# Order of the gate tiles in the up-projection stage of a quantized attention and feed-forward kernel

## What is computed

```python
x = act_qdq(x)                                   # x: layer-normed, 4096 rows of 512
up = act_qdq(x @ lpbq_dequant(w_up).T)           # 4096 x 1536
gate = act_qdq(x @ lpbq_dequant(w_gate).T)       # 4096 x 1536
sig = fixed_qdq_u16(jax.nn.sigmoid(gate))
gate = act_qdq(gate * sig)
o = act_qdq(gate * up)
return o @ lpbq_dequant(w_down).T
```

## Time and profile before

| | us |
|---|---|
| median of 3 runs (lowest, highest) | 898.39 (894.74, 899.74) |
| the profiled execution | 900.64 |
| its span, first to last instruction | 898.8 |
| TensorE busy in the span | 862.7 (96%) |
| VectorE busy | 691.9 (77%) |
| ScalarE busy | 586.1 (65%) |
| GpSimd busy | 194.9 (22%) |
| mean granted TensorE clock | 0.987 of full |
| DMA moved | 236.56 MB, mean 263 GB/s |

### The profile page before, as it was taken

How to read it: one execution, slowest core, us unless ns; L and a number is a source line. 1 busy time by engine, 2 the same in 40 slices (tenths; PEclk the granted TensorE clock), 3 DMA queues, 4 the chain that set the end, 5 groups by cost and what they waited for, 6 DMA issues and landing times.

```text
span 898.8 us, 11953 instructions
## 1 busy us (share of the span) xinstructions
PE 862.7 (96%) x4108; PEld 426.4 (47%) x4108; DVE 691.9 (77%) x965; ACT 586.1 (65%) x712; POOL 194.9 (22%) x170
## 2 busy tenths in 40 slices
PE   7999879999999999999999979999799989999998
PEld 5777554444444444444444424444344434444443
DVE  4889985565646559589997859757899997999992
ACT  2378776786654456599997758952789965555430
POOL 0099949499100196000000000000000000000000
PEclk9999979999999999999999989999999999999999
DMA  9822219756987549999459984799997887989872
GB/s 348 330 95 95 117 70 311 204 189 186 296 265 278 194 169 216 269 382 362 165 178 356 356 287 154 281 372 387 291 406 275 276 325 270 359 306 390 312 305 100
DMA packets 118402, 236.56 MB, mean 263 GB/s; under 512 B 47952, under 2 KB 57168, under 8 KB 116304
## 3 DMA queue, kind: packets, MB, share of 16 engines
q1 hardware_dynamic: 117200, 231.77, 73.4%
q10 hardware_dynamic: 1152, 4.19, 1.2%
HBM read 130.55 MB, written 95.42 MB: 251 GB/s over the span
## 4 chain that ended last, share of the span: by engine, by line
PE 66%; POOL 8%; DVE 7%; DMA 7%; issue 6%; ACT 4%; SPq 1%; ACTq 0%; DVEq 0%; POOLq 0%
PE ps L1097 23%; PE ps L1034 21%; PE ps L1150 14%; PE ps L1050 4%; PE ps L1177 3%; POOL big L866 2%; DMA big<-in_L_ffn_w_gate_dram 2%; DVE big L1948 2%; DVE big L1941 2%; DMA big<-gate_park 2%; DMA product_park<-big 1%; POOL big L823 1%; POOL big L817 1%; ACT big L1471 1%; PE ps L1167 1%
## 5 line engine op out<-in xcount | busy, mean ns | idle before, releaser
L1097 PE MATMUL ps<-big 128*128 (+1 forms) x1152 | 251.6, 382 | 6.2 <-ACT big L1195 6.2
L1195 ACT ACTIVATE big<-ps 128x1024 f32<-128x1024 f32 (+2 forms) x154 | 126.2, 830 | 138.6 <-PE ps L1034 62.4
L1034 PE MATMUL ps<-big 128*128 (+1 forms) x864 | 186.6, 379 | 0.3 <-DVE big L1725 0.3
L1097 PEld LDWEIGHTS ps<-big 128*128 128x128 f16 x1152 | 113.3, 98 | 144.4 <-issue 10.2
L1034 PEld LDWEIGHTS ps<-big 128*128 128x128 f16 x864 | 84.4, 98 | 102.3 <-DVE big L1725 0.8
L1150 PE MATMUL ps<-big 128*128 128x512 f16 x576 | 126.7, 383 | 2.3 <-DVE big L1969 2.3
L808 POOL PARTITION_ALL_REDUCE small<-small x8 | 3.0, 369 | 462.6 <-DVE small L1910 184.9
L1770 DVE TENSOR_REDUCE small<-big 128x1 f32<-128x1024 f32 x36 | 43.8, 1217 | 70.7 <-ACT big L1195 70.6
L1150 PEld LDWEIGHTS ps<-big 128*128 128x128 f16 x576 | 56.7, 99 | 71.7 <-issue 5.1
L1131 PE MATMUL ps<-big 128*128 128x512 f16 x384 | 85.1, 384 | 4.9 <-ACT big L1478 4.9
L1880 DVE CUSTOM_DVE_ANT_0 big<-big,small 128x1024 f32<-128x1024 int16 x48 | 61.6, 1284 | 7.3 <-DVE small L1874 0.5
(11 more groups left out here) (118 smaller groups left out, 1220.1 us busy)
## 6 DMA issues: line engine op xcount, KB each, us to landing
big<-up_park SPq DMA_DIRECT2D x90, 512.0 KB, 7.0
big<-gate_park SPq DMA_DIRECT2D x48, 512.0 KB, 6.5
up_park<-big SPq DMA_DIRECT2D x48, 512.0 KB, 5.0
gate_park<-big SPq DMA_DIRECT2D x36, 512.0 KB, 2.7
sign_park<-big SPq DMA_DIRECT2D x36, 256.0 KB, 2.7
big<-in_x_dram SPq DMA_DIRECT2D x8, 1024.0 KB, 18.2
x_park<-big SPq DMA_DIRECT2D x8, 1024.0 KB, 4.0
product_park<-big SPq DMA_DIRECT2D x16, 512.0 KB, 5.9
```

Source lines behind the costliest of these rows:

```text
L1034: mm = nc.tensor.matmul(unit_banks(n)[:, j], WG[:, x, a, k % 2, o:o + P], XT[:, g, b, k], start=(k == 0 and a + b == 0), stop=(k == KC - 1 ...
L1097: mm = nc.tensor.matmul(ps[:, b + j], WU[:, a, t // 3, k, t % 3], XT[:, g, c, k], start=(k == 0 and a + c == 0), stop=(k == KC - 1 and c = ...
L1195: return nc.scalar.activation(dst, src, ACT.Copy)
```

## The change

The bench tiles are worked from step 14 on, mixed with the shelf tiles, by a table `WORK` that gives the tile of each step. Signals count steps in place of tiles. `BENCH`, `BACK` and `HOLD` get other place numbers. A refill is issued two units after the unit that issued its product's store, in one run behind the shelf fetches and ahead of the stores of its unit. And the whole preparation of the up weights moves by one unit: loads, block maxima and scales by one flat unit, their high and low halves and the transposes by one quad.

```diff
-UP_AT = (1, 2, 3, 4)
-LOAD_AT = 27
-BLOCKS_AT = (29, 30)
-SCALE_AT = (31, 33)
+UP_AT = (0, 1, 2, 3)
+LOAD_AT = 26
+BLOCKS_AT = (28, 29)
+SCALE_AT = (30, 32)
...
-BENCH = (0, 1, 2, 3, 0, 1, 2, 3, 4, 5, 0, 1, 2, 3, 4, 5, 6, 7, 0, 1, 2, 3, 4, 5, 8)
+BENCH = (0, 1, 0, 1, 2, 3, 0, 1, 2, 3, 0, 1, 4, 5, 2, 3, 0, 4, 1, 6, 7, 5, 2, 3, 8)
 PARKED = 16
-BACK = (9, 6, 7, 0, 1, 2, 3, 4, 5, 8, 10, 11, 9, 6, 7, 0)
+BACK = (9, 0, 4, 1, 6, 7, 5, 2, 3, 8, 10, 11, 9, 0, 4, 1)
+BENCH_TURN = (14, 15, 20, 21, 23, 24, 26, 27, 29, 30, 32, 33, 34, 35, 36, 37) + tuple(range(39, 48))
...
-HOLD = (1, 2, 3, 4, 5, 8, 0, 6, 7, 9, 10, 11, 12, 13, 14, 15)
+HOLD = (6, 7, 5, 2, 3, 8, 0, 4, 1, 9, 10, 11, 12, 13, 14, 15)
 N_LD = 8
+
+
+def work_order():
+    kept = iter(range(KEPT))
+    return tuple(KEPT + BENCH_TURN.index(p) if p in BENCH_TURN else next(kept) for p in range(NU))
+
+
+WORK = work_order()
...
             def refill(i):
                 x = BENCH[i - KEPT]
                 later = [j for j in range(i + 1, NU) if j >= KEPT and BENCH[j - KEPT] == x]
-                if later:
-                    sp.wait_ge(p_st[(i - KEPT) % 4], 16 * ((i - KEPT) // 4) + 16)
-                    fetch_gate(later[0])
+                sp.wait_ge(p_st[(i - KEPT) % 4], 16 * ((i - KEPT) // 4) + 16)
+                fetch_gate(later[0])
...
             def park_product(i):
-                sp.wait_ge(a_mx, i + 1)
+                sp.wait_ge(a_mx, WORK.index(i) + 1)
...
                 if n:
                     park_up(n - 1)
                     next_gates(n)
-                for i in steps(n):
-                    if KEPT <= i < KEPT + PARKED:
-                        park_product(i)
-                    if KEPT < i <= KEPT + PARKED:
-                        refill(i - 1)
+                for t in steps(n - 2) if n > 1 else ():
+                    if KEPT <= WORK[t] < KEPT + PARKED:
+                        refill(WORK[t])
+                for t in steps(n):
+                    if KEPT <= WORK[t] < KEPT + PARKED:
+                        park_product(WORK[t])
...
-            def gate_abs(i):
+            def gate_abs(t):
+                i = WORK[t]
                 gate_fetched(act, i)
-                need(act, a_mx, i - 1)
-                nc.scalar.activation(g_abs[:, i % 2], place(i), ACT.Abs, scale=col["ginv"]).then_inc(abs_d, 1)
+                need(act, a_mx, t - 1)
+                nc.scalar.activation(g_abs[:, t % 2], place(i), ACT.Abs, scale=col["ginv"]).then_inc(abs_d, 1)
```

More of the change, by code:

```diff
@@ L1417, in take_up, with gate_int, sigmoid @@
                 copy(up_place(n), ps[:, b:b + 2].rearrange("p b w -> p (b w)")).then_inc(u_ev, 1)
-            def gate_int(i):
+            def gate_int(t):
+                i = WORK[t]
                 gate_fetched(act, i)
-                need(act, sig_d, i - 1)
-                nc.scalar.activation(g_int[:, i % 2], place(i), ACT.Copy, scale=col["ginv"]).then_inc(qact_d, 1)
-            def gate_abs(i):
+                need(act, sig_d, t - 1)
+                nc.scalar.activation(g_int[:, t % 2], place(i), ACT.Copy, scale=col["ginv"]).then_inc(qact_d, 1)
+            def gate_abs(t):
+                i = WORK[t]
                 gate_fetched(act, i)
-                need(act, a_mx, i - 1)
-                nc.scalar.activation(g_abs[:, i % 2], place(i), ACT.Abs, scale=col["ginv"]).then_inc(abs_d, 1)
-            def sigmoid(i):
-                if i % 3 == 0:
-                    act.wait_ge(qact_d, i // 3 + 1)
-                else:
-                    act.wait_ge(qdve_d, 2 * (i // 3) + i % 3)
-                act.wait_ge(abs_d, i + 1)
-                nc.scalar.activation(place(i), g_int[:, i % 2], ACT.Sigmoid, scale=col["gsc"]).then_inc(sig_d, 1)
+                need(act, a_mx, t - 1)
+                nc.scalar.activation(g_abs[:, t % 2], place(i), ACT.Abs, scale=col["ginv"]).then_inc(abs_d, 1)
+            def sigmoid(t):
+                if t % 3 == 0:
+                    act.wait_ge(qact_d, t // 3 + 1)
+                else:
+                    act.wait_ge(qdve_d, 2 * (t // 3) + t % 3)
+                act.wait_ge(abs_d, t + 1)
+                nc.scalar.activation(place(WORK[t]), g_int[:, t % 2], ACT.Sigmoid, scale=col["gsc"]).then_inc(sig_d, 1)
             def settle(q):
@@ L1449, in _ @@
                 if n < A_UNITS:
-                    for i in steps(n):
-                        if i % 3 == 0:
-                            gate_int(i)
-                        gate_abs(i)
-                        sigmoid(i)
+                    for t in steps(n):
+                        if t % 3 == 0:
+                            gate_int(t)
+                        gate_abs(t)
+                        sigmoid(t)
                 if n == B_UNIT:
@@ L1864, in up_max, with gate_int, sig_int, gate_product @@
                                         apply_absolute_value=True).then_inc(u_mx, 1)
-            def gate_int(i):
+            def gate_int(t):
+                i = WORK[t]
                 gate_fetched(dve, i)
-                need(dve, sig_d, i - 1)
-                nc.vector.tensor_scalar(g_int[:, i % 2], place(i), col["ginv"], None, ALU.mult).then_inc(qdve_d, 1)
-            def sig_int(i):
-                dve.wait_ge(sig_d, i + 1)
-                need(dve, a_mx, i - 1)
-                nc.vector.tensor_scalar(s_int[:, i % 2], place(i), 65536.0, 65535.0, ALU.mult, ALU.min).then_inc(r_d, 1)
-            def gate_product(i):
-                dve.wait_ge(abs_d, i + 1)
-                dve.wait_ge(r_d, i + 1)
-                s = i % 2
-                nc.vector.tensor_tensor_reduce(place(i), g_abs[:, s], s_int[:, s], 1.0, scol[:, s:s + 1],
+                need(dve, sig_d, t - 1)
+                nc.vector.tensor_scalar(g_int[:, t % 2], place(i), col["ginv"], None, ALU.mult).then_inc(qdve_d, 1)
+            def sig_int(t):
+                dve.wait_ge(sig_d, t + 1)
+                need(dve, a_mx, t - 1)
+                nc.vector.tensor_scalar(s_int[:, t % 2], place(WORK[t]), 65536.0, 65535.0, ALU.mult, ALU.min).then_inc(r_d, 1)
+            def gate_product(t):
+                dve.wait_ge(abs_d, t + 1)
+                dve.wait_ge(r_d, t + 1)
+                s = t % 2
+                nc.vector.tensor_tensor_reduce(place(WORK[t]), g_abs[:, s], s_int[:, s], 1.0, scol[:, s:s + 1],
                                                ALU.mult, ALU.max, scol[:, s:s + 1]).then_inc(a_mx, 1)
@@ L1902, in _ @@
                 if n < A_UNITS:
-                    for i in steps(n):
-                        if (i + 1) % 3 and i + 1 < NU:
-                            gate_int(i + 1)
-                        sig_int(i)
-                        gate_product(i)
+                    for t in steps(n):
+                        if (t + 1) % 3 and t + 1 < NU:
+                            gate_int(t + 1)
+                        sig_int(t)
+                        gate_product(t)
                 if n == B_UNIT:
```

## The result

| us | before | changed |
|---|---|---|
| median (lowest to highest) of 6 runs each | 899.10 (894.74 to 901.0) | 889.23 (888.38 to 890.84) |
| the profiled execution | 900.64 | 889.12 |
| its span | 898.8 | 887.3 |
| up stage, first to last matmul | 257.66 | 248.65 |
| DMA moved, mean GB/s | 236.56 MB, 263 | 236.56 MB, 267 |

The ratio of the runs is 0.990, 95% interval 0.9877 to 0.9924: 1.0% faster. In the changed kernel the lines are moved by some 10: the up matmul is L1106, the copies of up tiles L1204, the gate integer tiles L1432 (ScalarE) and L1881 (VectorE), the low halves L1669, the combines L1827.

What follows compares the result with a forecast made beforehand. The prediction took TensorE as the bound, with its up stage stopped by ScalarE's late copy. -9.02 for the up stage and +0.6 for the quads gave -8.4 us: 892.2 profiled, 890.0 as median, range 886 to 896.

Steps and rivals of the forecast that it cites:

- The up stage, -9.02 us: Up stage: TensorE's 6.23 us stop behind ScalarE's late copy and 2.8 us of low clock both go, -9.02 us.
- The cover of 14.5 us: Up stage: TensorE may run three units, 15.5 us, ahead; less the copy's 1.0 us, 14.5 us of ScalarE's lateness are covered.
- The relation of the prediction: Up stage: TensorE stops for what ScalarE's lateness exceeds 14.5 us; 20.7 us of waits give 6.2.
- The lateness left: Up stage, after the change: ScalarE 4.7 us late from transfer backlog, 12.7 at most with late refills; no stop.
- The 8.4 us at tile 39: Up stage: ScalarE's 8.4 us wait for tile 39, fetched one unit before its work, goes with the mixed order.
- ScalarE's sooner start, 0 in the sum: Start of the up stage: sooner up weights take 0 to 3.20 us off ScalarE's lateness; TensorE gains 0.
- The low halves, +0.6 us: Quads: sooner low halves fall more under GpSimd's rounding; stops of 1.9 us in place of 1.25, +0.6 us.
- rival 2: Quads: every pair of low halves in quads 0 to 2 is slow, +2.5 us, 892 us; chance 0.08.
- The second part: Units 33 to 47: up tile 38's copy, delayed by product fetches, stays hidden with 8 us left before unit 42.
- Rival 3: Second part of the up stage: a late up store or full DMA stops TensorE there instead, about 896; chance 0.06.
- Rival 4: Up stage: two units are too short for refills, gate tiles come late, the kernel is slower, 905.8; chance 0.06.
- Profiled against median: Whole kernel: the runs' median lies 2.25 us below the profiled execution, so 892.2 us profiled becomes 890.0.

Runs made afterwards that it cites:

- e11: The changed kernel with ScalarE's absolute values of step 30 (unit 20) made 16 times more, as lateness put in by hand; 901.3 us in one execution.
- e6: The changed kernel with refills three units behind the store in place of two; 897.39 us against 899.02 for the kernel before, ratio 0.9983.
- e5: The kernel before, old order and places, with only the refills moved two units behind their store; 901.15 us against 899.02, ratio 1.0032.
- e9: The changed kernel with ScalarE's absolute values of step 30 (unit 20) made 10 times more, as lateness put in by hand; 889.17 us in one execution.
- e1: The kernel before with only the places of tiles 39 to 42 changed, so tile 39's late fetch goes; 893.21 us against 897.54, ratio 0.9956.
- e3: The changed kernel with the up weights back at their old units; 889.41 us against 897.54 for the kernel before, ratio 0.9918.
- e2: The kernel before with only the up weights prepared a unit sooner; 894.42 us against 897.54, ratio 0.9971.
- e7: The changed kernel with loads, maxima and scales of the up weights at their old units, halves still sooner; 893.26 us against 899.02 before, ratio 0.9926.
- e8: The changed kernel with the up weights' halves back in quads 1 to 4, loads and scales still sooner; 890.0 us against 899.02 before, ratio 0.9885.
- e4: The changed kernel with refills one step behind the store, as in the kernel before; 890.79 us against 897.54 for the kernel before, ratio 0.9924.
- e12: The kernel before with new places for tiles 39 to 42 and up weights a unit sooner, old order and refills; 892.47 us against 898.43, ratio 0.9932.
- e10: The changed kernel with ScalarE's absolute values of step 30 (unit 20) made 13 times more, as lateness put in by hand; 896.38 us in one execution.

## Why the prediction was right, point by point

Forecast 890.0 (886 to 896), measured 889.23; 0.81 on faster. The mechanism is the one forecast, the stop behind ScalarE's late copy and the clock behind it. One term had the wrong sign, and some luck is in the closeness (last point).

- **The up stage, -9.02 us.** Right to the tenth: 257.66 to 248.65. That the stop was 6.2 us of lateness over the cover, and that a stop of this size costs 2.3 to 2.8 us of clock on top, is shown by e11, where both were made by hand; but a stop of 5.41 us (e6) cost 1.8, and e5, with two stops, paid twice, so "2.8 once" was one value of several. The cover of 14.5 us held in e9 to e11. The relation of the prediction was looser: it took the sum of ScalarE's waits for its lateness. In the kernel before this fits (20.7 waited, 20.6 us late at tile 26), because the 3.3 us left of the late start and the 0.33 us a unit won back cancel. In e5 and e6 the sums, 23.7 (23.1 for gate tiles, 0.6 for up stores) and 21.5 us, less 14.5 would give 9.2 and 7.0 us; the stops were 6.98 and 5.41.
- **The lateness left.** I had counted 4.7 us of backlog; the lateness is 4.6. That they meet is partly chance: 1.4 of the 4.6 us are there at every second tile from 16 to 24, and the one wait for a transfer is 3.1. The count for the kernel before was wrong: its SP code has 44 transfers in units 16 to 25, not 42, so 66.9 us in 51.8, and with tile 39 the sum is 23.5, not 20.4, against 20.7 waited. The count gives the direction; it was 2.8 us off there. The other estimate, a refill up to 0.5 us late at the median and 8 us in sum, was too dark: ScalarE never waited for a gate tile. The refills were issued sooner than I took from the old queue (where the up store stood behind a refill's wait), and product stores landed in 3.6 us at the median. The upper end of 12.7 us was not needed.
- **The 8.4 us at tile 39.** Right that it goes, wrong as a clean term: e1 gave back 3 of them as waits for up stores. The two causes, backlog and short distance, were not additive. Which share of the 20.7 us each has stays open.
- **ScalarE's sooner start, 0 in the sum.** Right for the changed kernel (e3), where TensorE has no stop to shorten. ScalarE's first gate instruction no longer waits for a transfer, and it began 4.2 us behind the stage's start in place of 5.2. The sooner weights by themselves were worth 3.1 us (e2), some 0.8 of it in the quads, which I would not have given them.
- **The low halves, +0.6 us.** This step failed in sign: the quads became 0.85 us shorter. I priced the pairs by their number under GpSimd, 0.6 us a quad, 1.9 us of stops in sum; they were 0.23, with eight long halves in place of the nine I had counted. The profiles show that one pair of 3.8 us makes the stop, and that ending the rounding 5 us sooner takes its usual place away (e7, e8). The error is 1.5 us. The Trainium skill, "SBUF — State Buffer", section "Who interferes with whom", calls the shared ports an exclusive lock. The durations agree that the two engines get in each other's way (a half takes 0.68 us alone and up to 1.96 under GpSimd); that the lock is exclusive no run here shows. It doesn't say which pair TensorE would feel, and rival 2 did not come.
- **The second part.** 8 us of margin forecast, 8.6 found. Rival 3 was seen only in e1 and e2 (0.8 to 1.0 us), where the first stop goes but ScalarE stays late.
- **Rival 4** needed the refill one unit later still (e6). Its 905.8 us is a slip: 898.4 + 16.2 - 9.0 is 905.6.
- **Profiled against median.** I took the profiled execution's 2.25 us over the median for a constant. It isn't one: the changed kernel's profiled execution took 889.12, at its median. Why the profile before was a long one is not shown. The low clock at the start of its down projection made that start 0.8 to 1.4 us longer than in the eight profiles without it, and would be a part; a longer stop than usual is the other candidate. The profiled difference was 11.5 us, the medians' 9.9. That the time came within 0.8 us of 890.0 is a little luck: the change was worth 1.5 us more than -8.4, about what the term of the quads was off, and half of that is hidden, because the base of 898.39 was the median of three runs and six give 899.10.

## What to carry to other kernels

Follow a stop of the busiest engine back to how late its helper is, and compare that with how far ahead the buffers let it run: lateness within the cover is free (11.8 us were), every us over it costs a us, and the clock may come on top (0 to 2.8 us here). Where such lateness comes from transfers, count them per unit from the issuing code against what a unit holds; moving the first use of a slot forward spreads the same bytes, and a refill may then be issued late enough that its wait never blocks the queue. In these runs a kernel near the edge of its cover also showed by its spread.

## What the runs showed of the hardware

- **The spread follows the stops.** The kernels without a stop stayed within 1.4 to 2.9 us over 4 to 6 runs each (the changed kernel, e3, e4, e7, e8); those with one ranged over 4.7 to 8.9 us (before 892.1 to 901.0 over all its runs, e1 890.9 to 896.9, e2 892.5 to 897.9, e5 899.5 to 904.2, e6 895.8 to 900.6), with more runs each. With six runs each it is 6.3 us before, 3.3 in e12, which is at the edge of its cover, and 2.5 in the changed kernel. That the stop itself varies from execution to execution is likely, but not shown.
- **What the clock costs behind a stop does not follow from the stop's length.** In the up stage the granted clock was 1.00 in the 5 to 6 us from the stops of 0.78 and 1.01 (e1), 1.88 and 0.80 (e2), 2.38 and 1.07 us (e10), and at most 0.4 us was lost besides. In the 5 us behind longer ones it was 0.66 and 0.50 (e5, 3.12 and 3.86 us, 4.6 us lost in the two), 0.67 (e6, 5.41, 1.8 lost), 0.56 (e11, 5.93, 2.3 lost) and 0.50, the 1.2 GHz level (before, 6.23, 2.8 lost). At the start of the down projection every profile has a stop of 2.00 to 2.42 us. In six of them (before, e5, e7, e8, e10, e12) the granted clock behind it was 0.66 to 0.69, and the 144 matmuls took 32.8 to 32.9 us; in the other eight it was 1.00, and they took 31.4 to 31.5, not counting a further stop of 0.29 to 0.74 us among them in six. A stop of 2.41 us is on both sides. e5 behind its first stop:

```profile
501.70:506.70 5.00, 5.00 (x16) 1.97 (x17) 4.71 (x8) 4.91 (x5) 0.00 (x0) 0.66 0.74 283
```

- **A stage's start has two lengths.** The flat stage's 864 matmuls, the same program in all, took 186.64 us in 9 of the 14 profiles and 188.33 in the other 5 (e4, e5, e7, e10, e11), nothing between. In e7 the granted clock from 125 to 140 us was 0.89. The profiles differ just ahead of the stage. In the five TensorE did the small matmuls from 126 to 130 us at a granted clock of 1.00, then stood 2.3 to 2.7 us, and from 130 to 135 us the clock was 0.66. In the nine it was 0.50 to 0.70 from 126 to 130, TensorE stood 0.3 to 1.1 us, and from 130 to 135 the clock was 0.93 to 1.00. Nothing in the kernels goes with it, so 1.7 us of any comparison of two single profiles may be this, and some 1 us more at the down projection; what sets it I did not find. The flat stage in the changed kernel and in e7:

```profile
130.05 186.64 PE L1043 MATMUL ps<-big 128*128 128x512 f16 x864 [0.71 <-DVE big L1736]
```

```profile
130.10 188.33 PE L1043 MATMUL ps<-big 128*128 128x512 f16 x864 [2.31 <-DVE big L1736]
```
